# Router logits with experts as output rows, weight turning moved between waits, and fewer gathers ahead of two barriers

## What is computed

```python
# layer 0, experts: one expert per token, at most 320 tokens each
logits = tokens @ gate_weight.T                 # 2048 x 8
top1 = argmax(logits); probs = softmax(logits)
ranks = cumsum(one_hot(top1)) - 1               # a token's place at its expert
out = gather -> gelu(x @ wi[e]) @ wo[e] -> scatter, times probs
# layer 1, attention part ("mixer"): a normed linear mixing whose
# token sums A (256 numbers) scale the output weights
q, k, v = ln(x) @ W_in; A from sum over tokens of k, v, rotary terms
y = q * (a function of A) @ W_out
# layer 1, experts: two experts per token, blocks of 128 slots
logits = h @ gate_w.T                           # 2048 x 8
out = (silu(x @ w1[e].T) * (x @ w3[e].T)) @ w2[e].T, weighted sum of two
```

## Time and profile before

| | |
|---|---|
| median of 3 executions | 1118.33 us |
| the profiled execution, its own time | 1126.37 us |
| its span, first to last instruction | 1124.5 us |
| PE busy | 986.2 us (88%), 10006 instructions |
| PE weight loads | 663.9 us (59%) |
| DVE (VectorE) busy | 640.0 us (57%) |
| ACT (ScalarE) busy | 517.6 us (46%) |
| POOL (GpSimd) busy | 299.4 us (27%) |
| mean granted TensorE clock | 0.923 |

### The profile page before, as it was taken

How to read it: one execution, slowest core, us unless ns; L and a number is a source line. 1 busy time by engine, 2 the same in 40 slices (tenths; PEclk the granted TensorE clock), 3 DMA queues, 4 the chain that set the end, 5 groups by cost and what they waited for, 6 DMA issues and landing times. The chain is left out here.

```text
span 1124.5 us, 24903 instructions
## 1 busy us (share of the span) xinstructions
PE 986.2 (88%) x10006; PEld 663.9 (59%) x10007; DVE 640.0 (57%) x1643; ACT 517.6 (46%) x805; POOL 299.4 (27%) x347
## 2 busy tenths in 40 slices
PE   7789899999999999977399999859677599999993
PEld 4334334445444444447277777746467599999993
DVE  5568999999799797743600000286574633333331
ACT  4434567777866865744122121376163233333330
POOL 2100510011001112220233423245810245544541
PEclk9988999999999999995699999979785699999997
DMA  5880000000000000009533785210533023222224
GB/s 183 187 159 3 2 2 3 2 3 3 2 3 2 3 3 2 3 2 312 193 100 109 206 253 154 45 45 1 169 94 112 19 43 52 47 47 51 46 43 93
DMA packets 63275, 78.81 MB, mean 70 GB/s; under 512 B 12096, under 2 KB 54976, under 8 KB 62736
## 3 DMA queue, kind: packets, MB, share of 16 engines
q1 hardware_dynamic: 50688, 61.54, 18.2%
q0 software_dynamic: 11968, 15.47, 8.5%
q10 hardware_dynamic: 528, 0.52, 0.1%
HBM read 58.12 MB, written 21.36 MB: 71 GB/s over the span
## 5 line engine op out<-in xcount | busy, mean ns | idle before, releaser
L594 ACT ACTIVATE k_prob<-f_s 128x1024 f32<-128x1024 f32 (+3 forms) x320 | 270.1, 896 | 121.6 <-PE f_s L432 121.0
L654 DVE TENSOR_REDUCE k_mpart<-f_r 128x1 f32<-128x512 f32 x384 | 250.7, 686 | 34.3 <-PE f_r L375 32.0
L375 PE MATMUL f_r<-k_ks,k_qs 112*32 112x512 bf16 (+3 forms) x2560 | 212.1, 357 | 19.8 <-DMA k_qs<-q_dram 7.8
L432 PE MATMUL f_s<-k_qs,k_ks 114*32 114x512 bf16 (+3 forms) x2560 | 175.1, 350 | 1.9 <-ACT k_prob L594 1.3
L850 POOL TENSOR_SCALAR_AFFINE_SELECT k_prob<-k_prob 128x256 f32<-128x256 f32 x128 | 51.2, 406 | 383.8 <-ACT k_prob L594 382.6
L375 PEld LDWEIGHTS f_r<-k_ks,k_qs 112*32 112x32 bf16 x2560 | 70.3, 96 | 136.9 <-DVE k_mpart L654 55.7
L448 PE MATMUL f_o<-k_prob,k_vaug 128*32 128x512 f32 (+3 forms) x1280 | 146.6, 531 | 1.5 <-POOL k_prob L850 1.4
L651 DVE CUSTOM_DVE_ANT_0 k_unread<-f_r,k_causal 128x128 bf16<-128x128 f32 (+3 forms) x256 | 121.2, 484 | 18.6 <-PE f_r L375 17.4
L432 PEld LDWEIGHTS f_s<-k_qs,k_ks 114*32 114x32 bf16 x2560 | 65.5, 97 | 78.3 <-issue 29.4
L2137 DVE TENSOR_TENSOR mid<-silu_g,e_u 128x512 f32<-128x512 f32 x39 | 26.8, 688 | 112.6 <-PE e_u L2039 111.6
L1327 DVE SCALAR_TENSOR_TENSOR outr<-p_o,k_w,k_mod 128x256 f32<-128x256 f32 x16 | 7.7, 484 | 133.7 <-PE p_o L1262 133.7
(11 more groups left out here) (379 smaller groups left out, 1326.2 us busy)
## 6 DMA issues: line engine op xcount, KB each, us to landing
k_w1T<-in_L_ffn_w_dram SPq DMA_DIRECT2D x18, 512.0 KB, 10.6
k_w1T<-in_L_ffn_wi_dram SPq DMA_DIRECT2D x8, 1024.0 KB
k_w1T<-in_L_ffn_wo_dram SPq DMA_DIRECT2D x8, 1024.0 KB
k_qs<-q_dram SPq DMA_DIRECT2D x6, 768.0 KB, 10.1
h_rows<-k_h SPq DMA_DIRECT2D x8, 512.0 KB, 5.6
sum<-k_x SPq DMA_DIRECT2D x8, 512.0 KB, 6.4
q_dram<-k_room SPq DMA_DIRECT2D x12, 256.0 KB, 8.8
k_rot_t<-in_L_ffn_w_dram SPq DMA_DIRECT2D x6, 512.0 KB, 5.0
```

What stands on the lines that cost most here:

```text
L375: last = nc.tensor.matmul(dst[32 * j:32 * (j + 1), :], qs[0:KROWS, c, GH * g + hs, q0:q0 + 32], ks[0:KROWS, QC * ck:QC * ck + w], start=Tr ...
L432: last = nc.tensor.matmul(sc[h % 2][32 * j:32 * (j + 1), i, off:QC], ks[0:KALL, k0:k0 + 32], qs[0:KALL, c, GH * g + 2 * pair + i, off:QC], ...
L594: nc.scalar.activation(prob[:, u % 2, 2 * pair:2 * pair + 2, off:QC], sc[h % 2][:, :, off:QC], ACT.Exp, scale=HD ** -0.5).then_inc(e_done, 1)
L654: nc.vector.reduce_max(mpart[:, s % 2, hs, t, ck:ck + 1], bank(r)[:, 0:w], AX.X).then_inc(ring_used[r % RING], 1)
```

## The change

Logits: `gT` becomes the stationary operand and 512 turned tokens the moving one, so that 8 experts are the output rows of a new bank `plT`; ScalarE copies these 8 rows to `lT`, and four small transposes of 8 x 128 per quarter bring them to `plog` as before. The same edit is made in both routers. In router 0 all modulation rows follow the rank. Each router issues one expert's or one block's gathers less, and the next phase issues them first. The turning order of experts becomes 0, 1, 2, 3, 5, 4, 6, 7 (`TURNED`), with raw places changed to suit: 6 halves go between the token sums and `A_rows`, 3 ahead of the combined weights, 3 behind them, none in the loop of output products, none at the start of router 1 and 12 behind its rank, with three and four banks in turn instead of two.

```diff
 HALVES = 6 * E
+TURNED = [0, 1, 2, 3, 5, 4, 6, 7]
...
-    if e < 4:
-        return k.flat1[:, 3072 * (4 + e):3072 * (5 + e)]
-    if e in (5, 6):
-        return k.flat1[:, 3072 * (e + 1):3072 * (e + 2)]
-    return k.rot_t[:, :, :, :].rearrange("p i s n -> p (i s n)")[:, 0:3072]
+    if e in (4, 7):
+        return k.rot_t[:, :, :, :].rearrange("p i s n -> p (i s n)")[:, 0:3072]
+    slot = {0: 4, 1: 5, 2: 6, 3: 7, 5: 4, 6: 7}[e]
+    return k.flat1[:, 3072 * slot:3072 * (slot + 1)]
...
-IN_TAIL, AT_START, REST = 12, 24, 40
+IN_TAIL, AT_START, IN_SUMS, IN_MIX = 12, 24, 30, 36
...
@@ router 0 (router 1 has the same logits, turn_logits, copy_logits) @@
             def logits(q):
                 pe.wait_ge(hT_ready, 2 * q + 2)
+                if q >= 1:
+                    pe.wait_ge(lT_ready, q)
+                for t in range(KH):
+                    last = nc.tensor.matmul(plT[0:E, :], gT[:, t, :], hT[:, q % 2, t, :],
+                                            start=(t == 0), stop=(t == KH - 1))
+                last.then_inc(lT_done, 1)
+
+            def turn_logits(q):
+
+                pe.wait_ge(lT_ready, q + 1)
                 for i in range(TQ):
-                    for t in range(KH):
-                        last = nc.tensor.matmul(plog[:, TQ * q + i, :], hT[:, q % 2, t, P * i:P * (i + 1)], gT[:, t, :],
-                                                start=(t == 0), stop=(t == KH - 1))
+                    last = nc.tensor.transpose(plog[:, TQ * q + i, :], lT[0:E, q % 2, P * i:P * (i + 1)],
+                                               k.ident[0:E, 0:E])
                 last.then_inc(log_done, 1)
...
                 if q >= 1:
                     logits(q - 1)
+                if q >= 2:
+                    turn_logits(q - 2)
             logits(NC - 1)
-            pe.wait_ge(wmod_in, 16)
-            mod_rows(0)
+            turn_logits(NC - 2)
+            turn_logits(NC - 1)
...
-            mod_rows(1)
-            mod_rows(2)
+            pe.wait_ge(wmod_in, 16)
+            for n in range(3):
+                mod_rows(n)
...
+            def copy_logits(q):
+                act.wait_ge(lT_done, q + 1)
+                if q >= 2:
+                    act.wait_ge(log_done, q - 1)
+                nc.scalar.copy(lT[0:E, q % 2, :], plT[0:E, :]).then_inc(lT_ready, 1)
...
             for q in range(1, NC):
                 turned(q)
+                copy_logits(q - 1)
+            copy_logits(NC - 1)
...
-            for e in range(2):
-                gather_rows0(nc, k, e)
+            gather_rows0(nc, k, 0)
...
@@ experts 0, GpSimd @@
+            gather_rows0(nc, k, 1)
             for e in range(E):
...
@@ router 1, TensorE @@
-            for n in range(REST, REST + 2):
-                turn_half(nc, k, ring[n % 2], n).then_inc(k.w_done, 1)
...
-            for n in range(REST + 2, HALVES):
-                if n == 6 * (E - 1):
-                    pe.wait_ge(k.raw_in[E - 1], 48)
-                pe.wait_ge(k.w_act, n - 1 - BY_DVE0)
-                turn_half(nc, k, ring[n % 2], n).then_inc(k.w_done, 1)
-            pe.wait_ge(k.w_act, HALVES - BY_DVE0)
+            pe.wait_ge(hT_ready, 2 * NC)
+            for n in range(IN_MIX, HALVES):
+                if n % 6 == 0:
+                    pe.wait_ge(k.raw_in[TURNED[n // 6]], 48)
+                if n >= IN_MIX + 4:
+                    pe.wait_ge(k.w_act, n - 3 - BY_DVE0)
+                turn_half(nc, k, ring[n % 4], n).then_inc(k.w_done, 1)
...
-            for b in range(2):
-                gather_row1(nc, k, b)
+            gather_row1(nc, k, 0)
...
@@ mixer, SP @@
+            sp.wait_ge(tp_done, KH * NC)
+            load_raw(sp, k, a, 5)
             sp.wait_ge(trig_ready, NT)
             load_raw(sp, k, a, 4)
             sp.wait_ge(A_done, 1)
-            load_raw(sp, k, a, 5)
             load_raw(sp, k, a, 6)
-            sp.wait_ge(k.w_done, 30)
+            sp.wait_ge(k.w_done, IN_MIX)
             load_raw(sp, k, a, 7)
...
@@ mixer, ScalarE @@
+            for n in range(AT_START, IN_SUMS):
+                keep_half(n)
             act.wait_ge(A_ready, 1)
...
-            for n in range(AT_START, REST):
+            for n in range(IN_SUMS, IN_MIX):
                 keep_half(n)
...
@@ mixer, TensorE @@
+            def turn_weights(n):
+                if n % 6 == 0:
+                    pe.wait_ge(k.raw_in[TURNED[n // 6]], 48)
+                if n >= AT_START + 3:
+                    pe.wait_ge(k.w_act, n - 2 - BY_DVE0)
+                turn_half(nc, k, ring2[n % 3], n).then_inc(k.w_done, 1)
+
+            pe.wait_ge(vals_ready, NT)
+            for n in range(AT_START, IN_SUMS):
+                turn_weights(n)
+
             pe.wait_ge(Arow_ready, 1)
...
             last.then_inc(A_done, 1)
+            for n in range(IN_SUMS, IN_SUMS + 3):
+                turn_weights(n)
             pe.wait_ge(wsc_ready, 2)
...
             last.then_inc(wc_done, 1)
+            for n in range(IN_SUMS + 3, IN_MIX):
+                turn_weights(n)
             pe.wait_ge(wc_ready, 1)
...
                 last.then_inc(y_done, 1)
-                n = AT_START + i
-                if n % 6 == 0:
-                    pe.wait_ge(k.raw_in[n // 6], 48)
-                if i >= 2:
-                    pe.wait_ge(k.w_act, n - 1 - BY_DVE0)
-                turn_half(nc, k, ring[n % 2], n).then_inc(k.w_done, 1)
...
@@ experts 1, GpSimd @@
                 if 2 <= b < NB:
                     pool.wait_ge(t_done, b - 1)
+                if 1 <= b < NB:
                     gather_row1(nc, k, b)
```

More of the change, by code:

```diff
@@ L888, in half_of @@
 def half_of(k, n):
-    return k.flat1[:, 512 * n:512 * (n + 1)]
+    at = 6 * TURNED[n // 6] + n % 6
+    return k.flat1[:, 512 * at:512 * (at + 1)]
 def turn_half(nc, k, bank, n):
-    e, m, half = n // 6, n // 2 % 3, n % 2
-    raw = raw_of(k, e)
+    raw, m, half = raw_of(k, TURNED[n // 6]), n // 2 % 3, n % 2
     for j in range(4):
@@ L1458, in turned, with copy_logits @@
                     if half == 0 and q >= 2:
-                        act.wait_ge(log_done, q - 1)
+                        act.wait_ge(lT_done, q - 1)
                     nc.scalar.copy(hT[:, q % 2, half, :], tp[q % 2][half][:, :]).then_inc(hT_ready, 1)
+            def copy_logits(q):
+                act.wait_ge(lT_done, q + 1)
+                if q >= 2:
+                    act.wait_ge(log_done, q - 1)
+                nc.scalar.copy(lT[0:E, q % 2, :], plT[0:E, :]).then_inc(lT_ready, 1)
             for q in range(3):
@@ L1465, in _ @@
             ln_normal(nc, act, k, 3, bias_ready, norm_ready)
-            turned(1)
-            for n in range(REST, REST + 2):
-                keep_half(n)
-            turned(2)
-            turned(3)
+            for q in range(1, NC):
+                turned(q)
+                copy_logits(q - 1)
+            copy_logits(NC - 1)
             act.wait_ge(delta_ready, 1)
             nc.scalar.activation(k.ex[:, :, :, :], pick[:, :, :, :], ACT.Exp).then_inc(exp_done, 1)
-            for n in range(REST + 2, HALVES):
+            for n in range(IN_MIX, HALVES):
                 keep_half(n)
@@ L1585, in phase_mix @@
         pk = [ps(f"k{s}", [P, D]) for s in range(2)]
-        pv = [ps(f"v{s}", [P, D]) for s in range(2)]
+        pv = [ps(f"v{s}", [P, QC]) for s in range(2)]
         pA, pw = ps("pA", [P, 4 * R2]), ps("pw", [P, QC])
-        ring = [pA, pw]
+        ring, ring2 = [pA, pw], [pw, pv[0], pv[1]]
         pwc, pbc, pAt = tp[0], tp[1][:, 0:D], tp[1][:, D:D + KH]
@@ L1825, in keep_half @@
                 act.wait_ge(k.w_done, n + 1)
-                nc.scalar.copy(half_of(k, n), ring[n % 2][:, :]).then_inc(k.w_act, 1)
+                bank = ring[n % 2] if n < AT_START else ring2[n % 3]
+                nc.scalar.copy(half_of(k, n), bank[:, :]).then_inc(k.w_act, 1)
             def outer(q):
@@ L1908, in keys_values @@
                         pe.wait_ge(used, i - 1)
-                    nc.tensor.matmul(out[i % 2][:, :], share[:, :], b_part[:, D * (n - 1):D * n], start=True, stop=False)
+                    nc.tensor.matmul(out[i % 2][:, 0:D], share[:, :], b_part[:, D * (n - 1):D * n], start=True, stop=False)
                     for t in range(KH):
-                        last = nc.tensor.matmul(out[i % 2][:, :], xnT[:, t, P * i:P * (i + 1)], w_in[:, t, D * n:D * (n + 1)],
+                        last = nc.tensor.matmul(out[i % 2][:, 0:D], xnT[:, t, P * i:P * (i + 1)], w_in[:, t, D * n:D * (n + 1)],
                                                 start=False, stop=(t == KH - 1))
```

33 lines of the change are left out of this document (22 added, 11 removed).

## The result

| | before | after |
|---|---|---|
| median of 4 executions each | 1118.57 us | 1107.37 us (1106.7 to 1108.22) |
| ratio | | 0.9883 (95% 0.9838 to 0.9929) |
| the profiled execution, its own time / span | 1126.37 / 1124.5 | 1106.7 / 1104.8 |
| mean granted clock | 0.923 | 0.945 |

The account below looks back on a forecast made before the run. TensorE was taken as the bound nearly everywhere except around both routers and the mixer's end, chains between engines at low clock. Router 0 -7.3, mixer -4.1, router 1 -4.6, together -16.0: 1102 us median, range 1096 to 1113.

Parts of the forecast that it names:

- Logits, -3.3 per router: Both routers: wide products with experts as rows bring VectorE's start on the logits 3.3 us earlier, through the higher clock.
- Rival A: Both routers: products with eight output rows don't lift the clock; +3.9 instead of -3.3 each, 1116.7 us; chance 0.12.
- let the clock rise near 520, at the end of the first logits: Router 0: the clock was taken to rise as the first quarter's wide products end, at 519.9 us.
- I carry the differences over: Whole sum: terms read against the profiled 1126.37 us were applied to the median of 1118.33, 8 us less.
- Modulation rows +0.3: Router 0: all 12 instructions now follow the rank; cost 0 to +1.7 us, taken as +0.3.
- Fewer gathers, -3.8 and -1.3: Ends of the routers: three of six gathers leave router 0, -3.8 us; one of two leaves router 1, -1.3.
- I take 0: Experts 0: moved gathers stay hidden unless rows land late in the full DMA; bounds 0 to +3.8 us, taken as 0.
- rival C: Router 0 into experts 0: gathers land late in the full DMA, +3.8 us, so -12.2 in all, 1106; chance 0.13.
- Mixer, -4.1: Mixer's end: VectorE starts the output loop 2.3 us earlier and the loop's four quarters save 1.8, total -4.1.
- rival B: Routers and mixer: neither narrow products nor transposes lift the clock; mixer -0.2, sum +2.3, 1120.6 us; chance 0.05.
- the loop's -1.8: Mixer's output loop: a quarter falls from 5.2 to 4.7 to 4.8 us, paced by VectorE; -1.8 over four quarters.
- Rival D: Mixer's output loop falls to the low clock through gaps in PE; +9.5 us, so -6.5 in all, 1111.8; chance 0.04.

Follow-up runs that it names:

- gathers_only: The kernel before with only three gathers moved in router 0 and one in router 1: 1114.83 us, ratio 0.9954.
- turning_only: The changed kernel with old logits and old gathers, leaving the new turning order and router 0's modulation rows behind the rank: 1119.22 us, ratio 0.9984.
- no_logits: The changed kernel with the old logits put back, modulation rows staying behind the rank: 1112.12 us, ratio 0.9906.
- after_third: The changed kernel again, unaltered, on the third chip: 1111.03 us, ratio 0.9885.
- logits_only: The kernel before with only the logits edits of both routers and router 0's modulation rows behind the rank: 1113.68 us, ratio 0.9943.
- mix_late: The changed kernel with the mixer's eight loads (3.4 MB) moved from router 0 to experts 0: 1107.76 us, ratio 0.9865.
- all_late: The changed kernel with idle products wherever PE idles in the touched stretches, and the mixer's eight loads moved to experts 0: 1103.73 us, ratio 0.9831.
- after_again: The changed kernel once more, unaltered, on the first chip beside its parts: 1109.18 us, ratio 0.9897.
- warm_before: The kernel before with three idle 512-column products of eight output rows ahead of each router's transposes: 1115.63 us, ratio 0.9958.
- short_gated: The changed kernel with GpSimd's gated additions cut from 256 to 8 channels for the last two quarters: 1106.65 us, ratio 0.9851.

## Why the prediction was right, and where it was off

**Logits, -3.3 per router: right mechanism, wrong instant, too small for this pair.** Measured -5.3 and -5.4 between the two profiles. Rival A's price did not come, and the products cost 0.43 each at clock 1, as taken from the modulation rows. The step that was off is "let the clock rise near 520, at the end of the first logits", 3.6 us after they begin. In router 0 it rose within 0.3 us of their beginning (513.0 for 513.2). I had read the instant off the wide modulation rows, where the clock came up only behind them. `gathers_only`, `turning_only` and `no_logits` show it lifted behind the first transposes of router 0 and then lost under the old logits. It is not so each time: router 0 of the kernel before and router 1 of those three did the same transposes and stayed at 0.50, and in router 1 of `after_third` the clock came up 2.5 us into the wide products, near where the forecast had it. What is the same in every profile of the changed kernel is that the dense wide stream, once up, holds it to the end of the logits.

**But the median got less from it than the pair of profiles.** First transposes to logits copy was 21.04 in the profile of before and 17.91, 17.92 and 17.91 in the three profiles with old logits and no idle products (`gathers_only`, `turning_only`, `no_logits`): so 3.1 of the 5.3 us belong to an execution in which the clock stayed at 0.50 to the end of the logits. Router 1 took 25.96 or 25.97 in all with old logits and no idle products. With 2.2 and 5.1 (`logits_only`'s 20.84) and the rank's 0.5 one gets 7.8, near the 7.5 measured for it alone. "I carry the differences over" was the weak step of the sum: it subtracts terms read in one execution from the median of others. Only one execution of the kernel before was profiled, so how often its router 0 stays cold is not shown. Its executions run from 1114 to 1128 us, and the profiled one is 8 us above the first median but 2 to 5 above those on the three later chips.

**Rank -0.5: right. Modulation rows +0.3: measured 0.** They ended 1.0 late, as the clock fell at 526.6, and the inversion, which then ran at 1.00, gave the 1.0 back before the gathers. In the two later profiles they weren't late at all (6.45).

**Fewer gathers, -3.8 and -1.3.** The size is right alone (-3.6), and -1.7 in router 1. The moved gathers stayed hidden: expert 1's transposes follow expert 0's first layer without idle time in `after` (560.95), as before. In the whole change router 0 gave only 1.4 to 2.2. The step that was off is "I take 0" for a late landing: rival C held in part, at 1.5 to 2.3 us of its 3.8. The argument against it used the times of before, where the last of three is issued after the loads; the logits' gain brought it to 542.5, under a share of 1.10. `mix_late` takes the loads away and the wait goes; `no_logits`, where router 0 is slower, has 6.25 with the loads in place. Here parts that each hold alone take from each other.

**Mixer, -4.1: -2.4 or -2.5 in seven profiles with its order, -1.4 in `after_third` and -1.9 in `all_late`.** From `A_rows`' product to the first bias addition before took 7.83; 5.72 when the clock was up (`turning_only`, `after_again`), -2.1 for a forecast of -2.3, and 6.87 where it fell behind the wait for `A_rows`. The clock is up at `A_rows`' product in all of them, where it was at 0.50 before, and in `after` it rose at 789.5, when PE had done only the six halves since 785.6: rival B is refuted. The mis-sized term is the loop's -1.8. VectorE's quarter is 4.84, a little over the forecast 4.7 to 4.8 and 0.37 under the old 5.21, which gives 1.5 over four. But the loop now starts earlier and GpSimd's chain doesn't, so a second bias addition meets it, and the earlier the start the more: with a start gain of 1.0 the loop gave 1.4, with 2.1 only 0.4, with GpSimd's chain cut short 2.3 (24.82 to 22.53; 0.9 of these come from the first addition, which GpSimd had slowed in the kernel before too). The second addition of 2.5 us instead of 1.2 is what took most of the loop's gain.

**Rival D, a slow loop: in one execution, for a piece.** In `after_third` PE idles behind the late second addition, and the clock is down for the third quarter's products:

```profile
806.00:808.50 2.50, 0.50 (x3) 0.25 (x2) 2.46 (x3) 0.00 (x0) 0.66 (x1) 1.00 0.29 98
809.80:812.60 2.80, 2.80 (x7) 2.25 (x8) 1.63 (x6) 0.00 (x0) 0.45 (x1) 0.50 0.00 0
```

That quarter took 7.08 us between bias additions, 6.15 in `after_again`: 0.9 us, a tenth of D's 9.5. In the kernel before, turned halves stood in that place.

**Router 1's halves, 0: right** (15.65 for 15.63).

**The total.** The parts alone measured 15.8 against a forecast of 16.0, but not in the forecast shares; the whole 11.2, 12.0 and 13.6, each beside its own executions of the kernel before. Summed by the marks, with router 0's logits at 17.91 for the kernel before, the touched stretches gave 14.3, 12.5 and 11.4 us in `after`, `after_again` and `after_third`, and the three parts alone 15.6. The shortfall against 15.6 is in the gathers under the loads (1.5 to 2.3 us), in router 1 where the clock rose late (up to 1.2 us more than in `logits_only`), and in `after_third`'s slow quarter of the loop. Untouched code adds scatter: experts 0 lasts 166.9 to 171.5 us over all kernels, in part by how long its first products stay at 0.50 (5.8 us and 17.95 to VectorE's first result in the kernel before, 8.8 us and 19.44 in `gathers_only`). That the parts' sum meets the forecast is partly luck: router 0's logits gave 2.2 and the mixer 2.5, under their 3.3 and 4.1, and router 1's logits gave 5.1, over their 3.3. The logits' share inside the whole isn't resolved: `no_logits` and `after_third` differ by 1.1 us at the median, with intervals of over 3 us on each side.

## What to carry to other kernels

When a low-clock stretch follows a rise, ask which instructions fail to hold the clock, not only which lift it: here a full PE whose products had 8 moving columns was no protection, and making those columns the output rows was. Read what an engine gains by moving earlier against what else is in flight at the new time: here the gathers met the weight loads, and VectorE met GpSimd. And take the terms of a sum for the median from more than one execution, where the clock's state differs between executions.

## What the runs showed of the hardware

- A PE that was 100% busy lost the clock when its stream was weight loads with 8 moving columns each between transposes: it fell at 515.8, 521.3, 516.2 and 515.1 us in router 0 of `gathers_only`, `turning_only`, `warm_before` and `no_logits`. The stream with 512 columns and eight output rows, once it ran at 1.00, kept it to the end of the logits in every profiled router.
- Transposes alone brought the clock up, at 513.0 above, at 789.5 in the mixer and at 732 in the earlier trace rows, but not each time: `no_logits` did transposes from 826.09 to 830.16 in router 1 and stayed at 0.50 until 856.4. The Trainium skill, "TensorE: Matmul & The Clock Gate", Part 4, says that the full clock doesn't engage for transposes; here the traces disagree.
- In the mixer's loop VectorE's additions and GpSimd's multiplications and additions on tensors in SBUF waited for each other rather than ran beside each other. The addition at 803.55 ends 1.09 after GpSimd's of 802.15 ended (804.50), and GpSimd's at 798.74 takes 3.33 rather than 2.35, beside VectorE's of 798.57, which ends at 799.86. The Trainium skill's "SBUF — State Buffer", section "SBUF: two separate sides", calls this an exclusive lock of a shared port pair for a whole instruction; by that rule, both lengths agree, and so does `short_gated` (1.22 and 1.21 with GpSimd idle).
